# Adding up a mixture of experts: two sums in HBM instead of four

## The reference

```
x = x + moe(layernorm(x))        # 64 experts of 192 hidden, 8 per token, capacity 128 rows per expert
x = x + attention(layernorm(x))  # one head of 256, 77 context rows
```

## Time and profile before

| what | value |
|---|---|
| median of 3 runs | 2209.79 us (2208.41 to 2211.33) |
| the profiled execution | 2211.68 us |
| its span, first to last instruction | 2209.9 us |
| mean granted TensorE clock | 0.955 |

### The profile page before, as it was taken

One profiled execution on the slowest core, in us unless ns is written; L12 is line 12 of the kernel. 1 busy time (PEld: TensorE's weight loads), 2 busy tenths in 40 slices (PEclk: granted clock), 3 DMA queues, 4 the chain that ended last, 5 costly groups with the idle time before them and its releaser, 6 DMA issues. The chain is left out here.

```text
span 2209.9 us, 39358 instructions
## 1 busy us (share of the span) xinstructions
PE 2042.1 (92%) x12891; PEld 1526.9 (69%) x12891; DVE 1098.7 (50%) x4126; ACT 937.1 (42%) x2965; POOL 613.7 (28%) x553
## 2 busy tenths in 40 slices
PE   7999999788999898899989799799997999599999
PEld 4776688555666555566645478578885677599998
DVE  5785344567777432777743368612222566322121
ACT  4564133255777420677742044322221666232332
POOL 0677466322222100222200002312223122221222
PEclk9999899789999999999999889899998999799999
DMA  8702799776700200000000181111122701466662
GB/s 287 296 20 64 235 338 333 207 234 214 299 12 11 68 1 27 18 10 11 11 8 1 62 286 43 43 35 32 32 59 54 249 35 40 166 184 184 175 184 56
DMA packets 162510, 255.35 MB, mean 116 GB/s; under 512 B 37484, under 2 KB 125967, under 8 KB 161270
## 3 DMA queue, kind: packets, MB, share of 16 engines
q1 hardware_dynamic: 132886, 224.62, 29.3%
q0 software_dynamic: 29424, 28.21, 7.2%
HBM read 165.95 MB, written 101.04 MB: 121 GB/s over the span
## 5 line engine op out<-in xcount | busy, mean ns | idle before, releaser
L2819 ACT ACTIVATE m3e_ht<-m3e_h_bank,m3w_b 128x128 f32<-128x128 f32 x312 | 89.2, 368 | 192.4 <-PE m3e_h_bank L2791 192.4
L3438 ACT ACTIVATE la_probs<-la_probs,la_nb,la_invnorm 128x256 f32<-128x256 f32 x256 | 150.2, 594 | 0.2
L2802 PE MATMUL m3e_y_bank<-m3w_w,m3e_ht 128*128 x624 | 141.0, 379 | 0.0
L2980 ACT ACTIVATE m2e_ht<-m2e_h_bank,m2w_b 128x270 f32<-128x270 f32 x128 | 62.3, 487 | 179.3 <-PE m2e_h_bank L2942 179.3
L981 POOL DMA_INDIRECT m_xbuf<-m0w_rows,m0w_slots x128 | 125.7, 982 | 39.7 <-issue 36.9
L2766 POOL DMA_INDIRECT out<-m3e_y,m3e_dest x39 | 60.4, 1548 | 239.0 <-DVE m3e_y L2854 225.1
L2802 PEld LDWEIGHTS m3e_y_bank<-m3w_w,m3e_ht 128*128 128x128 f32 x624 | 115.7, 190 | 14.1
L2917 POOL DMA_INDIRECT m_sum<-m2e_y,m2e_dest x48 | 70.2, 1462 | 197.2 <-DVE m2e_y L3028 186.2
L2831 DVE COPY m3e_xt<-m3e_turned_bank 128x256 f32<-128x256 f32 x39 | 16.6, 425 | 218.0 <-PE m3e_turned_bank L2779 218.0
L2942 PE MATMUL m2e_h_bank<-m2e_xt,m2w_w 128*128 128x270 f32 x512 | 121.9, 396 | 0.0
L2954 PE MATMUL m2e_y_bank<-m2e_ht,m2w_w 128*128 128x270 f32 x512 | 119.4, 391 | 0.0
(11 more groups left out here) (522 smaller groups left out, 4850.6 us busy)
## 6 DMA issues: line engine op xcount, KB each, us to landing
m3w_w<-in_m_w SPq DMA_DIRECT2D x32, 1024.0 KB, 6.5
m_xbuf<-all_zeros SPq DMA_DIRECT2D x38, 528.0 KB, 6.0
m2w_w<-in_m_w SPq DMA_DIRECT2D x16, 1024.0 KB, 12.7
m3e_w<-in_m_w SPq DMA_DIRECT2D x15, 1024.0 KB, 6.2
m0w_wgu<-in_m_gu SPq DMA_DIRECT2D x16, 768.0 KB, 14.3
m_xbuf<-all_zeros SPq DMA_DIRECT2D x16, 576.0 KB, 13.6
m0w_down<-in_m_down SPq DMA_DIRECT2D x23, 384.0 KB, 14.9
m_sum<-all_zeros SPq DMA_DIRECT2D x16, 512.0 KB
```

The source lines that it names most:

```text
L2802: last = nc.tensor.matmul(y_ps[t % 2][0:R, 0:D], h_t[t % 2][:, c, :], ahead.w2[:, bass.ts(e, 1), c, :].rearrange("p o f -> p (o f)"), star ...
L2819: last = nc.scalar.activation(h_t[t % 2][:, 4 * half + i, :], h_ps[t % 2][half][:, i * R:(i + 1) * R], m.act, bias=ahead.b1[:, bass.ds(e * ...
L3438: last = nc.scalar.activation(probs[u][:, hh, :], probs[u][:, hh, :], ACT.Exp, bias=nb[u][:, hh:hh + 1], scale=inv_norm[u][:, hh:hh + 1], ...
```

## The change

Two sums instead of four: the scatter of member i of each pair goes to `sums[i]`, and it waits for the scatter of member i of the pair before. Six pieces of zeros instead of sixteen are stored. `found_at` waits for the same scatters as before. The second attention loads x and one addend, adds once, and `local.shifted` now has room for four pairs of tiles, so that SP's loads wait for VectorE from pair 4 on.

```diff
-            self.sums = [... for i in range(4)]
+            self.sums = [... for i in range(2)]
-            self.summed = s.lasting_sems("summed", 4)
+            self.summed = s.lasting_sems("summed", 2)
...
-                sp.wait_ge(ahead.sum_zeroed, 16 * 16)
+                sp.wait_ge(ahead.sum_zeroed, 16 * 6)
...
         def addends(p, i):
-            at = 6 * (p % 2) + 2 * (i - 1)
+            at = 2 * (p % 4)
             return local.shifted[:, at:at + 2, :]
...
                 def load_x(p):
-                    if p >= 2:
-                        sp.wait_ge(x_summed, p - 1)
+                    if p >= 4:
+                        sp.wait_ge(x_summed, p - 3)
                     sp.dma_start(k.x[:, 2 * p:2 * p + 2, :], of_tokens(sums[0], p)).then_inc(x_in[p], 16)
-                    for i in range(1, 4):
+                    for i in range(1, 2):
                         sp.dma_start(addends(p, i), of_tokens(sums[i], p)).then_inc(x_in[p], 16)
...
-                for i in range(4):
-                    sp.wait_ge(summed[i], 16 * (M0.ntiles // 4))
+                for i in range(2):
+                    sp.wait_ge(summed[i], 16 * (M0.ntiles // 2))
...
                 def sum_x(p):
                     x = k.x[:, 2 * p:2 * p + 2, :]
-                    dve.wait_ge(x_in[p], 64)
-                    nc.vector.tensor_tensor(x, x, addends(p, 1), ALU.add).then_inc(summing, 1)
-                    nc.vector.tensor_tensor(addends(p, 2), addends(p, 2), addends(p, 3), ALU.add).then_inc(summing, 1)
-                    dve.wait_ge(summing, 2 * p + 4)
-                    nc.vector.tensor_tensor(x, x, addends(p, 2), ALU.add).then_inc(x_summed, 1)
+                    dve.wait_ge(x_in[p], 32)
+                    nc.vector.tensor_tensor(x, x, addends(p, 1), ALU.add).then_inc(x_summed, 1)
...
                     for i in range(2):
-                        j = 2 * (q % 2) + i
-                        if q >= 2:
-                            pool.wait_ge(summed[j], 16 * (q // 2))
-                        nc.gpsimd.indirect_dma_start(sums[j][:, :], ..., compute_op=ALU.add).then_inc(summed[j], 16)
+                        if q >= 1:
+                            pool.wait_ge(summed[i], 16 * q)
+                        nc.gpsimd.indirect_dma_start(sums[i][:, :], ..., compute_op=ALU.add).then_inc(summed[i], 16)
...
                     if q >= NY:
                         for i in range(2):
-                            dve.wait_ge(summed[2 * (q % 2) + i], 16 * ((q - NY) // 2 + 1))
+                            dve.wait_ge(summed[i], 16 * (q - NY + 1))
```

More of the change, by code:

```diff
@@ L221, in __init__ @@
         if m is M0:
-            self.sums = [k.nc.dram_tensor(f"{m.name}_sum{i}", (SUM_ROWS, D), F32, kind="Internal").ap() for i in range(4)]
+            self.sums = [k.nc.dram_tensor(f"{m.name}_sum{i}", (SUM_ROWS, D), F32, kind="Internal").ap() for i in range(2)]
             self.sum_zeroed, self.x_stored = s.lasting_sems("sumready")
-            self.summed = s.lasting_sems("summed", 4)
+            self.summed = s.lasting_sems("summed", 2)
             s = Scope(k, self.early, m.name + "w")
@@ L2079, in second_attention @@
         x_in, x1_in, offsets_in = s.sems("xin", NP), s.sem("x1in"), s.sem("offsetsin")
-        summing, x_first, x_summed = s.sem("summing"), s.sem("xfirst"), s.sem("xsummed")
+        x_first, x_summed = s.sem("xfirst"), s.sem("xsummed")
         kv3_in, qo3_in = s.sem("kv3in"), s.sem("qo3in")
@@ L2178, in sum_tile @@
                 def sum_tile(t):
[L2179 to L2184, removed]
+                    x = k.x[:, t, :]
+                    dve.wait_ge(x1_in if t else x_in[0], 32)
+                    nc.vector.tensor_tensor(x, x, addends(0, 1)[:, t, :], ALU.add).then_inc(x_summed if t else x_first, 1)
                 def sum_x(p):
                     x = k.x[:, 2 * p:2 * p + 2, :]
-                    dve.wait_ge(x_in[p], 64)
-                    nc.vector.tensor_tensor(x, x, addends(p, 1), ALU.add).then_inc(summing, 1)
-                    nc.vector.tensor_tensor(addends(p, 2), addends(p, 2), addends(p, 3), ALU.add).then_inc(summing, 1)
-                    dve.wait_ge(summing, 2 * p + 4)
-                    nc.vector.tensor_tensor(x, x, addends(p, 2), ALU.add).then_inc(x_summed, 1)
+                    dve.wait_ge(x_in[p], 32)
+                    nc.vector.tensor_tensor(x, x, addends(p, 1), ALU.add).then_inc(x_summed, 1)
                 def stats(t):
@@ L2506, in _ @@
                     for i in range(2):
-                        j = 2 * (q % 2) + i
-                        if q >= 2:
-                            pool.wait_ge(summed[j], 16 * (q // 2))
-                        nc.gpsimd.indirect_dma_start(sums[j][:, :], bass.IndirectOffsetOnAxis(dest[q % NY][:, i:i + 1], 0), y[q % NY][:, i, :], None,
-                                                     bounds_check=SUM_ROWS - 1, oob_is_err=True, compute_op=ALU.add).then_inc(summed[j], 16)
+                        if q >= 1:
+                            pool.wait_ge(summed[i], 16 * q)
+                        nc.gpsimd.indirect_dma_start(sums[i][:, :], bass.IndirectOffsetOnAxis(dest[q % NY][:, i:i + 1], 0), y[q % NY][:, i, :], None,
+                                                     bounds_check=SUM_ROWS - 1, oob_is_err=True, compute_op=ALU.add).then_inc(summed[i], 16)
             @block.tensor
```

## The result

The changed kernel takes 2269.98 us (median of 4 runs, 2265.46 to 2274.22) against 2210.56 us before on the same chip: ratio 1.0269, 95% interval 1.0245 to 1.0293, so 59 us slower. The forecast was 2237 with a range of 2208 to 2264. The direction is right, the size is not.

The account below looks back on a forecast made before the run. TensorE was taken to bound the experts, with full DMA engines beside it; waiting scatters would take over. Experts +37.2 and second attention -9.7 gave +27.5 us, from the median of 2209.8 to 2237 us, range 2208 to 2264.

Parts of the forecast that it names:

- start, 6 links: Narrow experts, first steps from one pair's scatter to the next pair's, beside full DMA queues: 8.1 us each, 48.6 us.
- middle, 17 links: Narrow experts, up to link 23, loads coming at the scatters' pace: 6.2 us each, 105.4 us.
- tail, 8 links: End of the narrow experts, scatters without loads beside them: 3.9 us each, 31.2 us.
- experts against 154.2: Narrow experts to the second attention's first load: that load at 451.0 instead of 413.83, +37.2 us.
- second attention: Half the loads, one add instead of three: 4.4 us earlier start, then -2.7 and -2.6 along the tiles; -9.7 us.
- middle link of 6.2 us: Scatter-to-scatter step in the experts' middle, taken near the 6.4 us median landing, between 5.2 and 7.0 us.
- restart of 0.1: Experts' scatters: time from a landing to the next scatter's start, about 0.1 us in each link.
- the same formula: Experts' middle: landing between 3.7 and 8.0 by share of time with loads; T = 3.8 + 4.3 x 5.2/T, 7.0 us.
- head start of the scatters: Experts' middle: loads released by the later scatter's landing must still be issued and begun, so links are under 7.0 us.
- stays at 8 us: Rival, experts: a pair's loads fall on the scatters each time, 23 links at 8.1 us; 2254 to 2275, chance 0.17.
- TensorE's clock: Rival, experts' middle: idling lowers the clock, 6.7 us per link, +8.5, 2246; chance 0.12 shared with the short attention gain.
- The zeroing: First attention: ten of sixteen 512 KB stores go, covered by SP's wait of 102.0 us; 0.

Follow-up runs that it names:

- serial run: The changed kernel with one wait more: every scatter waits for the scatter just before it, of either member; 2411.82 us in its one run.
- without the loads: The changed kernel, but weights of pairs 9 to 31 are not loaded and those there are used again; 2205.2 us, ratio 0.9981.
- the wait alone: The kernel before with its four sums, and each scatter also waiting for the same member's scatter one pair earlier; 2282.34 us, ratio 1.0340.
- the attention alone: The kernel before with its scatters and four sums, its second attention loading and adding only the first two; 2200.8 us, ratio 0.9958.

## Why the prediction was wrong in size

*The mechanism: right.* The wait for the previous pair's scatter is the whole loss, the bound moves from TensorE to GpSimd's scatters, the result buffers hand it on to VectorE, TensorE and SP, and it ends with the loads. The terms of the sum against what the run gave:

| term | predicted | measured |
|---|---|---|
| start, 6 links | 48.6 | 46.0 |
| middle, 17 links | 105.4 | 135.0 |
| tail, 8 links | 31.2 | 37.4 |
| last scatters to the first load | 6.25 | 6.4 |
| experts against 154.2 | +37.2 | +70.6 |
| second attention | -9.7 | -9.6 |

*The step that failed: the middle link of 6.2 us,* made of a landing of about 6.1 and a restart of 0.1. It is 7.94, of 7.2 and 0.75; over 17 links that is 19 us of landing and 11 of restart, 30 of the 33 us by which the experts were missed. Two things stood behind it.

The restart of 0.1 us had no row, and no run shows such a value. The trace of before has a row for it: VectorE's copy ends at 301.62 and the scatter that waits for it starts at 302.38.

```profile
300.75 0.87 DVE L2682 TENSOR_SCALAR m0e_y<-m0e_y_bank,m0e_weight 128x256 f32<-128x256 f32 x2
...
302.38 1.54 POOL L2510 DMA_INDIRECT m_sum<-m0e_y,m0e_dest  x1 [1.37 <-DVE m0e_y L2682]
```

As long as TensorE was the bound it cost nothing; in a chain of scatters it is paid at every link, in the tail too: 8 x 0.65 = 5.2 of the 6.2 us that the tail is over.

The landing was taken from the share of time with loads in flight, as if loads and scatters met by chance. With 0.75 in place of 0.1 the same formula gives T = 4.45 + 22.4 / T, 7.45 us. The 0.5 us from there to 7.94 are put down to their not meeting by chance; the rows above show that they do not, but no run moves the loads while leaving everything else as it is. That the later scatter's landing releases a pair's loads was seen, and taken for a head start of the scatters, a reason to go down from 7.0 to 6.2. It works the other way: the scatter that the link waits for starts 0.3 us after the first of its loads and flies through the whole burst. The serial run shows it with the members exchanged: 6.7 us for the one that starts with the loads, 3.7 for the one behind them.

*The rival that came true* is the landing that "stays at 8 us", from 7.2 us per link on: 2254 to 2275, by its own reason, that the loads of a pair fall on the scatters each time. It had 0.17. The landing alone is less than 8; restart and landing together are 7.94.

*The estimate by the Trainium skill,* "DMA: Bandwidth & Descriptors", section "Anatomy of one DMA — SWDGE (gpsimd) path" (2.3 us for these bytes), is not reached even without loads: 3.7 us in the changed kernel's tail, 3.8 without the loads. The measurement decides, for a scatter that adds in HBM.

*TensorE's clock:* in the middle its granted clock fell from 1.00 to 0.90, over 181 us in which it was idle for 40, but its waits of 40.3 us for the result buffers show that it was not the bound.

*The second attention: right in sum,* with some luck, for its two parts were off by about as much, in opposite directions. The first normalised tile that hangs on pair 1 comes 8.0 us after the first load, not 13.6: 5.6 us gained for 4.4. The remaining 4.0 stand against 5.3: for the same 349 instructions TensorE is busy 55.13 us at a granted clock of 0.84; over 414 to 499 us before the change it was

```profile
414.00:499.00 85.00, 59.40 (x349) 43.09 (x349) 57.05 (x225) 35.47 (x129) 18.15 (x32) 0.77 0.78 264
```

So up to 4 of the 9.6 us may hang on the clock of one execution. TensorE's waits for the normalised tile, from the third on, fell as well, from 3.7 to 0.3 us (the two of 1.35 are gone); the runs do not part the two. Over all profiles the attention takes 73.9 to 76.0 us with two sums (five), and 85.5 and 81.8 with four and the loads of before (two: before, and the wait alone); the gain is between 6 and 12, and 0.42%, 9 us, by the medians of the attention alone.

*The zeroing: right, 0.* From 80 to 120 us the DMA share falls from 0.48 to 0.12, and TensorE's busy time is 39.72 us both times.

*Open:* the profiled execution of after is only 54.4 us over that of before, less than its 61.0, since the stages behind the attention, which the change leaves alone, took 1702.7 us instead of 1710.6. In the ten experiments they took 1702.9 to 1710.5, with two, three and four sums; what sets it was not looked for.

## What to carry to other kernels

A wait that costs nothing while another engine is the bound has a full price per turn once it closes a loop: landing, plus the time from a semaphore to the next start, both read from rows. Ask next what the same event releases: a chain that lets loose its own loads flies beside them every time, and the mean load of the DMA engines gives too small a price (7.45 us against 7.94 here). And look for the gain apart from the loss: about half of what two sums brought the attention, by the medians, was to be had with four, by fewer and larger loads.

## What the runs showed of the hardware

- From the event that releases it (a landing, or the end of VectorE's copy) to the start of an indirect DMA on GpSimd about 0.75 us pass: 344.69 after a landing at 343.9, 302.38 after a copy that ends at 301.62.
- The adding scatter of 128 KB lands in 3.7 us without loads beside it and in 8.0 (median) at a DMA share of 1.07; behind a burst that has just ended it is 3.7 again (serial run).
- Back to back, GpSimd issues such scatters every 1.85 us (three sums and twelve buffers: 1.87 on average over twelve).
- Scatters into four parts of one array go on side by side as into four arrays: the experts took 154.2 us either way.
